# ACT fetches 16 rows a step in every layer of a four-layer graph network; layer 2b shifts before it adds; relation maps on both halves of TensorE's rows

## The reference

```python
# layer 0 (GIN)
h = x + segment_sum(x[src], dst);  y = elu(h @ W1 + b1) @ W2 + b2
# layer 1 (message passing)
msg = relu(concat(x[src], x[dst], edge_attr) @ mW1 + mb1) @ mW2 + mb2
y = relu(concat(x, segment_sum(msg, dst)) @ uW1 + ub1) @ uW2 + ub2
# layer 2 (two SAGE layers: 2a, and behind a batch norm 2b)
h = l2norm(mean(x[src], dst) @ Wl1 + b1 + x @ Wr1)
h = relu(gamma * (h - mu) * rsqrt(var + eps) + beta)      # over all nodes
y = l2norm(l2norm(mean(h[src], dst) @ Wl2 + b2 + h @ Wr2) + x)
# layer 3 (relations)
y = segment_sum(x[src] @ weight[edge_type], dst)
```

## Time and profile before

| | us |
|---|---|
| median of 3 runs | 9605.86 (9603.74 to 9610.63) |
| the profiled execution, its own time | 9613.65 |
| its span, first to last instruction | 9611.7 |
| gathers of layer 0 | 2.8 to 1916.3 |
| layer 1 | 1936.1 to 3842.4 |
| layer 2a | 3859.8 to 5742.9 |
| layer 2b | 5757.7 to 7663.0 |
| layer 3 | 7719.1 to 9600.6 |

### The profile page before, as it was taken

One profiled execution on the slowest core, in us unless ns is written; L12 is line 12 of the kernel. 1 busy time (PEld: TensorE's weight loads), 2 busy tenths in 40 slices (PEclk: granted clock), 3 DMA queues, 4 the chain that ended last, 5 costly groups with the idle time before them and its releaser, 6 DMA issues.

```text
span 9611.7 us, 127811 instructions
## 1 busy us (share of the span) xinstructions
PE 4955.0 (52%) x23790; PEld 4259.7 (44%) x23791; DVE 2604.7 (27%) x6055; ACT 1301.8 (14%) x2785; POOL 7166.3 (75%) x7594
## 2 busy tenths in 40 slices
PE   4555555566666666344444445666666633333333
PEld 3444444456666665333333334555555522222222
DVE  2222222234444444111121223333333311111111
ACT  1111111111111111000000002222222200000000
POOL 7777777777777777777777777777777667777777
PEclk7555555577777777555555555555555555555555
DMA  3111111133333333111111112222232211111111
GB/s 76 34 34 34 35 34 35 34 93 96 95 94 96 95 95 92 29 31 32 31 32 32 31 31 72 82 83 81 80 84 80 76 32 30 30 30 30 30 30 29
DMA packets 460729, 529.13 MB, mean 55 GB/s; under 512 B 220578, under 2 KB 287616, under 8 KB 459848
## 3 DMA queue, kind: packets, MB, share of 16 engines
q0 software_dynamic: 242880, 349.17, 16.2%
q1 hardware_dynamic: 93785, 88.18, 3.3%
q10 hardware_dynamic: 123247, 83.52, 3.0%
HBM read 442.93 MB, written 77.29 MB: 54 GB/s over the span
## 4 chain that ended last, share of the span: by engine, by line
POOL 70%; issue 23%; PE 3%; ACTq 2%; ACT 1%; DVE 1%; SPq 0%; DMA 0%; POOLq 0%; DVEq 0%
POOL G L520 70%; PE PH L1282 1%; PE PAG L1282 1%; ACTq L383 1%; ACTq L391 1%; PE NA L1282 0%; SPq L422 0%; ACT G L755 0%; PE NB L1282 0%; DVE G L1153 0%; ACT STG L680 0%; ACT Y L663 0%; ACT XT L590 0%; DMA rel_tab<-STG 0%; DVE Y L1038 0%
## 5 line engine op out<-in xcount | busy, mean ns | idle before, releaser
L1282 PE MATMUL PAG<-OH,G 128*64 128x96 f32 (+2 forms) x12126 | 2294.9, 382 | 3742.0 <-DMA G<-rel_tab,IDX 988.0
L1282 PEld LDWEIGHTS PAG<-OH,G 128*64 128x64 f32 (+2 forms) x12126 | 2097.5, 253 | 3971.2 <-issue 3425.2
L520 POOL DMA_INDIRECT G<-rel_tab,IDX x1507 | 1421.9, 944 | 515.7 <-issue 459.6
L520 POOL DMA_INDIRECT G<-far_tab,SRC x1527 | 1440.8, 944 | 485.3 <-issue 465.5
L520 POOL DMA_INDIRECT G<-h_tab,SRC x1524 | 1439.4, 944 | 480.7 <-issue 463.5
L520 POOL DMA_INDIRECT G<-in_x,SRC x1525 | 1440.6, 945 | 475.2 <-issue 464.6
L520 POOL DMA_INDIRECT G<-x_tab,SRC x1507 | 1423.4, 945 | 477.1 <-issue 459.7
L941 DVE TENSOR_TENSOR AGG<-AGG,PAG 64x96 f32 (+2 forms) x980 | 245.8, 251 | 5434.9 <-PE PAG L1282 5432.6
L905 DVE TENSOR_TENSOR OH<-CONST,DREL 128x768 f32<-128x768 f32 x980 | 926.9, 946 | 3.2 <-issue 2.3
L1282 PE MATMUL PAG<-OH,HT 128*128 128x96 f32 x3126 | 615.7, 378 | 583.2 <-ACT HT L748 579.0
L1282 PEld LDWEIGHTS PAG<-OH,HT 128*128 128x128 f32 x3126 | 572.8, 283 | 630.3 <-ACT HT L748 625.3
(11 more groups left out here) (173 smaller groups left out, 3896.4 us busy)
## 6 DMA issues: line engine op xcount, KB each, us to landing
GROWS<-x_tab SPq DMA_DIRECT2D x4096, 0.2 KB
GROWS<-rel_tab SPq DMA_DIRECT2D x4096, 0.2 KB
GROWS<-in_x SPq DMA_DIRECT2D x3584, 0.2 KB
GROWS<-h_tab SPq DMA_DIRECT2D x3456, 0.5 KB
rel_tab<-STG ACTq DMA_DIRECT2D x200, 250.0 KB
GROWS<-far_tab SPq DMA_DIRECT2D x3072, 0.5 KB
GROWS<-x_tab ACTq DMA_DIRECT2D x3072, 0.2 KB
GROWS<-rel_tab ACTq DMA_DIRECT2D x3072, 0.2 KB
```

What stands on the lines that cost most here:

```text
L520: pool.indirect_dma_start(out=G[:, h, j, 0:tabs[p].shape[1]], out_offset=None, in_=tabs[p], in_offset=bass.IndirectOffsetOnAxis(ap=numbers ...
L1282: return nc.tensor.matmul(dst, lhsT, rhs, start=start, stop=stop, skip_group_check=True)
```

## The change

ACT takes every eighth super in every layer. It issues 16 rows at the end of its work on each super, and loads 32 registers at a time. Layer 0 begins with super 41, the others with super 9. So ACT has 20, 24, 24, 24 and 24 supers, where it had 10, 12, 24, 12 and 24; SP keeps 28, 24, 32, 27 and 32. In layer 2b VectorE shifts the rows of super s ahead of the add of super s-1, and TensorE waits for that add by a wait of its own. The relation maps of a unit use the two halves of TensorE's rows: `XT` holds the first 125 nodes on partitions 0 to 63 and the other 125 on 64 to 127, `wrel` is loaded twice, and the four products alternate between the halves.

```diff
-ACT_STEPS = [16, 16, 8, 16, 8]
-ACT_AT_ONCE = 16
+ACT_STEPS = 8
+ACT_AT_ONCE = 32
+ACT_PIECE = P // ACT_STEPS
-ACT_SUPERS = [range(49 if p == 0 else n + 1, SUPERS - 1, n) for p, n in enumerate(ACT_STEPS)]
+ACT_SUPERS = [range(41, SUPERS - 1, ACT_STEPS)] + [range(ACT_STEPS + 1, SUPERS - 1, ACT_STEPS)] * 4
...
-        wrel = sb("wrel", [D, R * D])
+        wrel = sb("wrel", [2 * D, R * D])
-        XT = sb("XT", [D + 1, UNIT])
+        XT = sb("XT", [P, UNIT])
...
                 if stage == 3:
-                    flip_copy(3, u)
+                    act.wait_ge(flipped[3], u + 1)
+                    nc.scalar.activation(XT[:, 0:HALF], PT[:, 0:HALF], ACT.Copy).then_inc(flip_copied[3], 1)
                     tile_free(3, u)
...
                     for k in range(4):
-                        a, b = k // 2, k % 2
+                        a, b = k % 2, k // 2
...
-                piece = P // ACT_STEPS[p]
-                at = (s + ACT_STEPS[p] + 1 - ACT_SUPERS[p][0]) * piece
+                at = (s + ACT_STEPS + 1 - ACT_SUPERS[p][0]) * ACT_PIECE
...
-                for i in range(piece):
+                for i in range(ACT_PIECE):
...
+                        if p == 3:
+                            shift_straight(s, h)
                         if s:
                             add_straight(p, s - 1, starts[s - 1], m)
...
-                        if p == 3:
-                            shift_straight(s, h)
...
                 elif p == 3:
                     pe.wait_ge(bn_relu, s + 1)
+                    pe.wait_ge(added, SUPERS * p + s + 2)
...
-                    flip(3, XS, D)
+                    for a in range(2):
+                        last = mm(PT[a * D:(a + 1) * D, 0:HALF], XS[0:HALF, a, :], IDENT[0:HALF, 0:HALF])
+                    last.then_inc(flipped[3], 1)
                     pe.wait_ge(flip_copied[3], u + 1)
-                    for k in range(4):
-                        c = slice(k % 2 * 512, k % 2 * 512 + 512)
-                        mm(PH[k // 2][0:HALF, c], XT[0:D, half(k // 2)], wrel[:, c]).then_inc(l3_map, 1)
+                    for b in range(2):
+                        c = slice(b * 512, b * 512 + 512)
+                        for a in range(2):
+                            k = slice(a * D, (a + 1) * D)
+                            mm(PH[a][0:HALF, c], XT[k, 0:HALF], wrel[k, c]).then_inc(l3_map, 1)
```

More of the change, by code:

```diff
@@ L322, in gnn_kernel @@
             (ub1c[:, :], ub1), (uw2[:, :], uW2), (wl1[:, :], Wl1), (wr1[:, :], Wr1), (gam[:, :], gamma),
-            (bet[:, :], beta), (wl2[:, :], Wl2), (wr2[:, :], Wr2), (wrel[:, :], Wrel),
+            (bet[:, :], beta), (wl2[:, :], Wl2), (wr2[:, :], Wr2), (wrel[0:D, :], Wrel), (wrel[D:2 * D, :], Wrel),
         ]
@@ L1439, in node1 @@
                     pe.wait_ge(flip_copied[1], u + 1)
-                    mm(NA[:, 0:UNIT], u1[:, :], XT[:, :], stop=False)
+                    mm(NA[:, 0:UNIT], u1[:, :], XT[0:D + 1, :], stop=False)
                     for a in range(2):
```

## The result

The changed kernel takes 9952.1 us in the median of 4 runs (9949.31 to 9956.3), the kernel before 9607.27 us (4 runs) on the same chip: a ratio of 1.0359, with a 95% interval of 1.0341 to 1.0377. It is slower by 345 us; 337 us were forecast, 9943 us in all.

What follows compares the result with a forecast made beforehand. GpSimd's gathers bound the kernel before; ACT's order would bind layer 2b after. ACT's 46.7 against 38.9 us over 46.75 cycles gives +365 us, layers 0 and 1 -27.5: +337, median 9943 us; 8 in 10 range 9760 to 10040.

Steps and rivals of the forecast that it cites:

- GpSimd's row of gathers as the bound: All layers before, only just in 2b: gathers at 1.25 us set the pace; 34 fewer would spare 42.5 us.
- ACT's cycle: Layer 2b, four supers: ACT's own order grows from 35.7 to 46.7 us against GpSimd's 38.9, adding 365 us.
- The rows: ACT in layer 2b: 64 row fetches a cycle take 21.1 us where 32 took 10.7, +10.4 us a cycle.
- the waits for VectorE and NB: ACT in layer 2b: waits of 1.6 us and part of 3.5 us for the shift go, and 0.66 us for NB.
- The load of 32 registers: ACT, two loads a cycle: each 0.95 us longer than 16 registers' 1.23, +1.9 us a cycle, bounds 0 and 2.0.
- The maps: Layer 2b relation maps on both row halves: if they overlap, ACT saves 0 to 2.4 us a cycle, taken as 0.5.
- The drain: ACT's register load behind four 250 KB stores ends when they drain, about 10 us after the first; sooner stores gain little.
- Shift ahead: VectorE in layer 2b: shifting before the add costs nothing, gains nothing alone, and takes VectorE out of the loop.
- the end of layer 2b: The tail of layer 2b gets up to 2 us shorter from the maps on both halves.
- GpSimd as the only bound in layer 2b: Rival: ACT stays under GpSimd's pace in layer 2b and the 42.5 us come whole, 9563 us; chance 0.11.
- The cheap cycle: Rival: maps overlap, load waits a fixed time behind the last store, 32 registers cost like 16; 9770 to 9840 us, 0.14.
- Layer 0 did not turn to ACT: Rival: layer 0 also becomes bound by ACT if half its idle times stay, +228 us, 10170 us in all; chance 0.05.

Runs made afterwards that it cites:

- a2: Changed kernel with the relation maps as before, all on the lower half of the rows, one behind the other: 9981.1 us, ratio 1.0387.
- a8: Changed kernel with each of the four relation maps stored twice, the second time to a table nothing reads: 10369.1 us, ratio 1.0790.
- a5: Changed kernel with the 32 registers loaded right behind the relu, ahead of the unit's stages and the four map stores: 9741.1 us, ratio 1.0138.
- b3: Kernel before with only the relation maps put on both halves of TensorE's rows: 9599.0 us, ratio 0.9988.
- a3: Changed kernel with VectorE's shift behind the add again in layer 2b: 9953.9 us, ratio 1.0360.
- b2: Kernel before with only the shift ahead of the add in layer 2b: 9599.2 us, ratio 0.9990.
- b1: Kernel before with one edit, ACT issuing 16 rows a super in layer 2b too: 10046.8 us, ratio 1.0457.

## Why the prediction was right

- **GpSimd's row of gathers as the bound.** Right. 1515 gathers in layer 0 took 1901.8 us, with one wait at its start as before; layers 0 and 1 give -26.4 us, for -27.5 forecast.
- **ACT's cycle.** It was summed to 46.7 us from the earlier trace rows; the cycle shown is 46.56 us and the median of the layer 46.7. The rows (21.1 forecast, 21.05 measured) and the waits for VectorE and NB, which went, are as put. Layer 2b grew by 374.7 us, for 365. Counted by units it comes out the same way: the 47 distances from one copy of XT to the next, 3 of which span three supers and not four, have a mean of 45.9 us where it was 38.0, and 47 x 7.9 = 371.
- **The load of 32 registers.** Put at 2.15 us for ACT (1.2 and 0.95 more) from SP's duration; measured 2.21 us in the median. The rule of the Trainium skill, "Runtime: NRT & Kernel Launch", the note on TENSOR_LOAD, of about 200 ns a register would have given over 4 us. The trace disagrees, at 0.06 us for each further one; the page speaks of loads from HBM, and these are from a tile in SBUF.
- **The maps.** TensorE's overlap was left open and is shown, 3.59 us for 7.19, in agreement with "up to 2x" in "TensorEngine Tiling (Array Packing)", Theoretical Speedup, of the Trainium skill. Its gain for ACT was put at 0.5 us a cycle between 0 and 2.4; a2 shows 0.6.
- **The drain.** Argued from the end of the load behind the first store; a8 shows that more stores make it longer and a5 that a load ahead of them doesn't have it. "A drain is not shortened by issuing it sooner" holds in the main: with the stores 2.26 us closer together the load ended 0.4 us sooner (a2 against the changed kernel) and 1.0 us sooner (b3 against before). What I had not put is that starts of stores and row fetches are slowed too, and that loads of SP are held like ACT's.
- **Shift ahead.** That it costs nothing and gains nothing holds in the changed kernel (a3). But the prediction had this edit take ACT's waits for VectorE out of the cycle (1.6 us and part of 3.5), and this step was wrong: in a3 they are gone without it, because ACT comes later. The sum came out right since the waits go either way.
- **The term that was mis-sized: the end of layer 2b.** "Up to 2 us shorter" was put for the maps. The wait for the relation table fell by 10.0 us in the changed kernel, 16.9 us with the maps alone and 9.6 us with the shift alone. TensorE's last sums of the layer, before and in the changed kernel, tell the two parts of it:

```profile
7691.95 1.60 PE L1282 MATMUL PAG<-OH,G 128*128 128x96 f32 x6
8030.73 1.05 PE L1283 MATMUL PAG<-OH,G 128*128 128x96 f32 x6
```

  They end 30.6 us behind the last gather before and 23.2 us now, 21.0 us in b2 and 16.7 us in b3. From there to the first gather of layer 3 it is 25.5 us before and 25.6 in b2, and 23.0 us in the changed kernel and 22.5 in b3, with the maps on both halves. So the work on the last unit itself is 2.5 us shorter, about what was put, and the larger part is that the engines stand less far behind the gathers. I treated that lateness as free because GpSimd doesn't wait for it, and forgot that the end of a layer does. That it fell because the edits shorten the loop of ACT and TensorE, which the earlier trace rows showed to be about as long as GpSimd's, is argued and not shown.
- **The rivals.** GpSimd as the only bound in layer 2b is refuted by b1. The cheap cycle is refuted in both parts, by a2 and by the load's duration. Layer 0 did not turn to ACT: its idle time shrank as it had to. Before, ACT stood 7.7 us idle behind the rows in stage 0; now from 1012.87 to 1015.37, 2.5 us:

```profile
1007.61 5.26 ACTq L392 DMA_DIRECT2D GROWS<-in_x  x16
1015.37 0.83 ACT L604 ACTIVATE POS<-NA,b1c 128x250 f32<-128x250 f32 x2 [7.42 <-DVE NEG L1054]
```

## What to carry to other kernels

An engine's busy share says nothing of its room when it also starts DMAs and loads registers: follow its program through one full cycle, take out only the waits that end on others, and compare what is left with the pace of the bound. Moving work off the bounding engine pays as long as that sum stays below; at 35.7 of 38.9 us there was room for 3 us, not for 11, and the rest came back as waits of the bound. A lateness that the buffers hide all through a stage is paid once, at its end. And a wait that goes when its engine becomes the late one needs no edit to remove it.

## What the runs showed of the hardware that was not expected

A load of 32 registers took 6.0 to 8.9 us on ACT in place of 2.15 with ACT's four stores of 250 KB ahead of it (48 loads of the changed kernel), and 6.0 to 11.3 us on SP, which had started none of them (20 loads). With eight stores their starts took up to 4.1 us in place of 0.3 (a8), and 16 row fetches right behind four stores took 7.5 us in place of 5.2 (a5, medians of the layer).

With the maps on both halves TensorE's granted clock in layer 2b is higher: 0.56 on the mean in b3 against 0.51 before. The window of layer 2b in b3:

```profile
5754.60:7658.20 1903.60, 1001.28 (x4254) 811.05 (x4254) 681.83 (x1694) 455.09 (x962) 1438.96 (x1524) 0.56 0.27 80
```

In b2, which has the maps as before:

```profile
5758.00:7661.30 1903.30, 1245.36 (x4254) 951.96 (x4254) 679.18 (x1695) 459.95 (x962) 1438.69 (x1524) 0.51 0.27 80
```

It shows in the sums behind the maps. The stretch of these sums in the changed kernel, with the columns of the earlier trace rows:

```profile
6714.10:6716.10 2.00, 1.99 (x18) 1.82 (x16) 0.00 (x0) 1.29 (x3) 1.44 (x2) 1.00 0.35 95
```

The same sums before:

```profile
6753.80:6757.50 3.70, 3.70 (x17) 3.47 (x16) 0.00 (x0) 0.60 (x1) 2.78 (x4) 0.50 0.46 153
```

The granted clock is 1.00 there, 2.4 GHz, and was 0.50, 1.2 GHz; the 16 matrix products take 2.0 us, not 3.7. What the engine did before it rose is 3.5 us of maps on both halves, at 0.54; before, it was 7.1 us of maps on one half, at 0.50, and the clock stayed low. So it did in a2, the changed kernel with the maps on one half: 0.50 in the maps and in the sums behind them. Why the one lifts it and not the other was not tried apart.
